# A one-core perceiver layer: steps without loops, 64-byte token list entries, a second attention by own sequence, and a new order of five steps

## What is computed

```python
def layer(x, ctx):
    # 1: cross attention with random features
    n = layernorm(x)
    K, V = ctx @ Wk + bk, ctx @ Wv + bv
    K_hat = cos(K @ Wr + br)                                   # 64 x 257 x 256
    x = x + softmax((n @ Wq + bq) @ K_hat.T) @ V
    # 2: attention inside one sequence of 32 tokens, top 8 earlier tokens by similarity
    h = layernorm(x)
    A = top8_of_strictly_earlier_tokens(h @ h.T)
    s = where(A, (h @ W_q.T) @ (h @ W_k.T).T / sqrt(32), -1e9)
    msg = softmax(s) @ h
    x = x + gelu((mix * h + (1 - mix) * msg) * gain + bias) * scale
    # 3: mixture of 8 experts, the best one for each token
    n = layernorm(x); p = softmax(n @ W_route); e = argmax(p)
    return x + max(p) * (gelu(n @ W1[e] + b1[e]) @ W2[e] + b2[e])
```

## Time and profile before

| | us |
|---|---|
| runs of before | 519.25, 520.58, 527.82 |
| median | 520.58 |
| the profiled execution's own time | 522.69 |
| its span (first to last instruction) | 520.6 |
| TensorE busy | 456.7 (88%) |
| VectorE busy | 286.1 (55%) |
| ScalarE busy | 268.8 (52%) |
| GpSimd busy | 186.8 (36%) |

### The profile page before, as it was taken

The page is one execution under the profiler, slowest core; times in us unless marked ns, Lnnn a source line. Parts: engine busy times, 40 slices in busy tenths (PEclk is TensorE's granted clock), DMA queues, the critical chain, the costliest instruction groups (busy, mean ns, idle before and its releaser), DMA issues. The chain is left out here.

```text
span 520.6 us, 10379 instructions
## 1 busy us (share of the span) xinstructions
PE 456.7 (88%) x2839; PEld 336.9 (65%) x2840; DVE 286.1 (55%) x904; ACT 268.8 (52%) x587; POOL 186.8 (36%) x326
## 2 busy tenths in 40 slices
PE   4889999999999759999999167985977999999992
PEld 3545565666666426666665055885967899999992
DVE  1556778888898548898898334763321121222220
ACT  2366768877788527788777233534213132233320
POOL 2732235334653414653545043442231332223210
PEclk9799999999999969999999768899999899999997
DMA  8612522325415305415551090353549556555300
GB/s 229 206 39 93 171 92 64 110 93 173 132 44 171 91 1 171 132 43 170 171 174 42 0 362 22 99 207 118 146 124 373 150 203 212 206 178 171 125 0 1
DMA packets 49106, 69.13 MB, mean 133 GB/s; under 512 B 8702, under 2 KB 38976, under 8 KB 48932
## 3 DMA queue, kind: packets, MB, share of 16 engines
q1 hardware_dynamic: 42820, 59.12, 34.6%
q0 software_dynamic: 3520, 8.23, 4.6%
q10 hardware_dynamic: 2720, 1.26, 0.9%
HBM read 62.20 MB, written 7.30 MB: 133 GB/s over the span
## 5 line engine op out<-in xcount | busy, mean ns | idle before, releaser
L1311 PE MATMUL pK<-stage,Wkr 128*128 128x512 f32 x256 | 126.2, 619 | 9.8 <-DVE stage L739 9.2
L1154 ACT ACTIVATE XF<-pT,b_now 128x128 f32<-128x128 f32 x184 | 52.6, 368 | 119.3 <-PE pT L1334 82.3
L1334 PE MATMUL pT<-XF,stage 128*128 128x128 f32 x736 | 92.0, 285 | 4.5 <-DMA stage<-in_L_ffn_W_dram 4.5
L1334 PEld LDWEIGHTS pT<-XF,stage 128*128 128x128 f32 x736 | 90.9, 201 | 6.9 <-issue 5.8
L1348 PE MATMUL pK<-W,XF 128*128 x368 | 87.0, 387 | 2.9 <-issue 1.3
L1348 PEld LDWEIGHTS pK<-W,XF 128*128 128x128 f32 x368 | 68.7, 193 | 12.6 <-issue 3.9
L1311 PEld LDWEIGHTS pK<-stage,Wkr 128*128 128x128 f32 x256 | 45.3, 196 | 48.7 <-issue 48.2
L356 POOL TENSOR_SCALAR ve<-mv 128x1 f32<-128x1 f32 x48 | 13.3, 276 | 157.2 <-DVE mv L662 157.1
L1135 ACT ACTIVATE stage<-pK,bkr 128x512 f32<-128x512 f32 x64 | 42.9, 689 | 34.5 <-PE pK L1311 33.0
L1142 ACT ACTIVATE stage<-stage 128x512 f32<-128x512 f32 x64 | 40.5, 633 | 20.4 <-DVE stage L734 20.2
L734 DVE TENSOR_TENSOR stage<-stage 128x512 f32<-128x512 f32 x64 | 47.7, 746 | 1.2
(11 more groups left out here) (194 smaller groups left out, 696.2 us busy)
## 6 DMA issues: line engine op xcount, KB each, us to landing
stage<-in_L_ffn_W_dram SPq DMA_DIRECT2D x23, 1024.0 KB
stage<-in_ctx_dram SPq DMA_DIRECT2D x32, 512.0 KB, 4.9
W<-in_L_ffn_W_dram SPq DMA_DIRECT2D x8, 1024.0 KB, 5.9
rows_by_token<-rows_out SPq DMA_DIRECT2D x16, 256.5 KB
ctx_last<-in_ctx_dram SPq DMA_DIRECT2D x64, 32.0 KB, 4.0
X<-in_x_dram SPq DMA_DIRECT2D x1, 1792.0 KB, 7.5
stage<-in_L_ffn_b_dram SPq DMA_DIRECT2D x1, 1024.0 KB, 9.0
token_i<-tokens_by_expert SPq DMA_DIRECT2D x23, 0.5 KB
```

Of the source, the lines that this page charges most:

```text
L1154: ins = act.activation(f_hT[b][:, n * P:(n + 1) * P], pT[i][:, (n % 4) * P:(n % 4 + 1) * P], ACT.Gelu, bias=b1_now[:, b, n:n + 1])
L1311: mm = pe.matmul(pK[r][:], Wkr[:, c, r * P:(r + 1) * P], ctx_T[:, c, half * 512:(half + 1) * 512], start=c == 0, stop=c == DC - 1)
L1334: mm = pe.matmul(pT[i][:, (n % 4) * P:(n % 4 + 1) * P], W1[q][:, c, n * P:(n + 1) * P], f_inT[:, q % 2, c * P:(c + 1) * P], start=c == 0, ...
```

## The change

1. Loops are gone: `run_steps` writes out all 21 steps, and the 16 late blocks are written out. The helpers for register values (`settle`, `in_register`, `upto`) go, and the waits on constants that `settle` made.
2. An entry of the token list is 16 int32 (64 bytes) in place of one. The start fills 1.18 MB of DRAM in place of 74 KB. `token_now`, `token_i` are 16 wide.
3. The second attention works on each sequence's own 32 columns. Similarity is 2 x 4 matmuls (128 rows, 32 x 32), scores 4 matmuls of 32 rows, `msg` 4 matmuls of 32 rows and 256 columns; queries and keys are made untransposed (64 columns), scaled in the weights, and transposed by VectorE in blocks (`qkT`); ScalarE's two copies go. All VectorE tiles there have 32 columns.
4. A new order in steps 16 to 20 on GpSimd, SyncE, VectorE and TensorE.

```diff
 def run_steps(eng, step):
-    for s in range(PEELED):
-        step(s // 2, s % 2, s // 4, s // 2 % 2)
-    with eng.Fori(0, (NG - 2 - PEELED) // 4) as i:
-        for k, half, kp in ((3 + 2 * i, 1 + i, 1), (4 + 2 * i, 2 + i, 0)):
-            step(k, 0, half, kp)
-            step(k, 1, half, kp)
-    for s in range(NG - 2, NG + STAGES):
+    for s in range(NG + STAGES):
         step(s // 2, s % 2, s // 4, s // 2 % 2)
-        by_expert = nc.dram_tensor("tokens_by_expert", [(E + 1) * TOK, 1], I32, kind="Internal").ap()
+        by_expert = nc.dram_tensor("tokens_by_expert", [(E + 1) * TOK, ENTRY], I32, kind="Internal").ap()
...
@@ gpsimd, step
                 if s in (17, 19):
-                    scatter(*routed, half - 2 + kp)
...
+                if s == 20:
+                    count_pair(routed[0])
+                    gather(5)
+                    gather(6)
...
                 if two:
                     rstd(two[0], mv2, ve2, rs2, "mv2_r", "ve2_r", "rs2_r")
                 if s == 16:
-                    gather(1)
+                    gather(0)
...
                 if s == 16:
-                    gather(2)
+                    gather(1)
+                if s in (17, 19):
+                    scatter(*routed, half - 2 + kp)
                 if four:
                     rstd(four[0], mv3, ve3, rs3, "mv3_r", "ve3_r", "rs3_r")
-                if routed and not parity:
+                if routed and not parity and s < 20:
                     count_pair(routed[0])
+                if s == 16:
+                    gather(2)
...
-                if s == 15:
-                    gather(0)
...
-                    gather(5)
-                    gather(6)
@@ sync
+                if j in FIRSTS:
+                    sp.wait_ge(S["expert_r"], FIRSTS.index(j) + 1)
-            load_tokens(0, 0, FIRSTS[1])
             sp.wait_ge(S["pv"], NG - 1)
             stream_w1(0, 0, 0)
+            load_tokens(0, 0, FIRSTS[1])
...
             keep(5, 2)
-            load_tokens(1, 3, 5)
             sp.wait_ge(S["pv"], NG)
             stream_w1(*ring(3))
+            load_tokens(1, 3, 5)
...
             keep(7, 2)
+            stream_w1(*ring(EARLY))
             load_tokens(3, EARLY, EARLY + SLOTS)
@@ vector, step
+                    v.transpose(qkT[:], p_qk).then_inc(S["qk_cp"], 1)
-                if s == 16:
-                    begin(0)
...
+                if s == 16:
+                    begin(0)
...
-                if s == 16:
-                    begin(1)
...
+                if s == 16:
+                    begin(1)
@@ tensor
-                pe.matmul(p_msg, attT[:], h[:, b, :], start=True, stop=True).then_inc(S["msg_mm"], 1)
+                for j in range(BG):
+                    own = slice(j * T, (j + 1) * T)
+                    mm = pe.matmul(p_msg[own, :], attT[own, :], h[own, b, :], start=True, stop=True,
+                                   skip_group_check=True)
...
+                    mm = pe.matmul(p_scoreB[own, :], qkT[own, 0:H], qkT[own, H:2 * H], start=True, stop=True,
+                                   skip_group_check=True)
...
                 if s == 20:
+                    up(*ring(4), 1)
                     pe.wait_ge(S["logits_r"], NG)
                     rank(routed[0])
-                    up(*ring(4), 1)
...
-                        mm = pe.matmul(p_sim, hT[:, c, :], hT[:, c, :], start=c == 0, stop=c == DC - 1)
+                        for j in range(BG):
+                            own = hT[:, c, j * T:(j + 1) * T]
+                            mm = pe.matmul(p_sim[j * T:(j + 1) * T, :], own, own, start=c == 0, stop=c == DC - 1,
+                                           skip_group_check=True)
...
-                        mm = pe.matmul(p_qk, WqkT[:, c, :], hT[:, c, :], start=c == 0, stop=c == DC - 1)
+                        mm = pe.matmul(p_qk, hT[:, c, :], WqkT[:, c, :], start=c == 0, stop=c == DC - 1)
```

More of the change, by code:

```diff
@@ L42 @@
 UNPICKED = -1.0e9
-OUTSIDE = -3.0e38
 STAGES = 5
-PEELED = 6
 def at_least(eng, sem, count):
-    if not isinstance(count, int) or count > 0:
+    if count > 0:
         eng.wait_ge(sem, count)
[L55 to L68, removed]
 def groups(k, parity, behind):
     g = 2 * k + parity - behind
-    if isinstance(g, int) and not 0 <= g < NG:
+    if not 0 <= g < NG:
         return None
@@ L82, in pair, with run_steps @@
     q = k - 3
-    if isinstance(q, int) and not 0 <= q < NG // 2:
+    if not 0 <= q < NG // 2:
         return None
     return q, 2 * ((kp + 1) % 2)
-def run_steps(eng, step):
-    for s in range(PEELED):
+def run_steps(step):
+    for s in range(NG + STAGES):
         step(s // 2, s % 2, s // 4, s // 2 % 2)
-    with eng.Fori(0, (NG - 2 - PEELED) // 4) as i:
-        for k, half, kp in ((3 + 2 * i, 1 + i, 1), (4 + 2 * i, 2 + i, 0)):
-            step(k, 0, half, kp)
-            step(k, 1, half, kp)
-    for s in range(NG - 2, NG + STAGES):
-        step(s // 2, s % 2, s // 4, s // 2 % 2)
[L100 to L112, removed]
 def perceiver_layer(nc, a, out):
@@ L587, in keep @@
                                  ).then_inc(rows_st[r0 // 2], 16)
-            for g in range(2, PEELED):
+            for g in range(2, NG):
                 next_group(g, g % 2)
@@ L939, in step @@
                     end(1)
-                if routed and not parity and (s is None or s < 18):
+                if routed and not parity and s < 18:
                     route(routed[0])
@@ L1079, in step @@
                     plan_rows(3)
-            run_steps(v, step)
+            run_steps(step)
             def late_block(j, q, turn):
-                if not isinstance(j, int) or j + 1 < NBLK:
-                    bias1(*following(j, q, turn))
-                    in_T(*following(j, q, turn))
+                if j + 1 < NBLK:
+                    bias1(*ring(j + 1))
+                    in_T(*ring(j + 1))
                 bias2(j, q, turn)
@@ L1092, in _ @@
                 end(j)
-            run_late(v, late_block)
+            for j in range(EARLY, NBLK):
+                late_block(*ring(j))
         @block.scalar
@@ L1247, in _ @@
                 late_block(*ring(j))
-            run_late(act, late_block)
+            for j in range(EARLY, NBLK):
+                late_block(*ring(j))
         @block.tensor
@@ L1528, in step @@
                     rank(routed[0])
+                if s == 16:
+                    up(*ring(0), 1)
+                    down(0, 0, (0,))
+                    in_T(*ring(1))
                 if s == 1:
```

228 lines of the change are left out of this document (107 added, 121 removed).

## The result

The changed kernel takes 481.15 us (median of 4 runs, 478.69 to 483.07) against 522.17 us beside it (519.25 to 527.82): a ratio of 0.923, 95% interval 0.915 to 0.931. The profiled execution took 483.07 us, its span 481.3 us, so the trace has 39.3 us less than the 520.6 of before.

The account below looks back on a forecast made before the run. TensorE was taken to bound full steps and late blocks, waits the stretch between; 12.3 (loops) + 0 (attention) + 22.8 (steps 16 to 20) + 8.3 (late blocks) = 43.4 us, giving 479.3 profiled, 477 at the median, range 465 to 498.

Parts of the forecast that it names:

- rival 3: Straight code stalls once where the loop's jump did, so all 12.3 us stay: 490 us; chance 0.06.
- Rival 1: Scattered 64-byte entries land no sooner, in 10 us, costing 14 us in step 16 and later blocks: 491 us; chance 0.18.
- four terms of 0.60, 0.37, 0.40 and 0.60 us: TensorE's second attention per full step: similarity, queries and keys, scores, `msg`; sum 1.97 us as before, so no gain.
- Rivals 2 and 4: Second attention: `msg` tiles run one after another, 497 us, chance 0.11; each small matmul drains the array, 540 us, chance 0.04.
- the sign of being right: Full steps of 16.2 to 16.6 us with TensorE busy throughout.
- the four named waits: TensorE idle for `h` (10.80, 3.77 us), W1 of block 0 (2.19) and `rank` (3.46) in steps 16 to 20: 20.2 us.
- The clock's 5.8 come back with the long waits: Steps 16 to 20: three half `up` slowed by low clock behind long waits recover, gaining about 5.8 us.
- the small waits: Steps 16 to 20: the rest of 16.2 us beyond the long waits, less 5.8 of clock, kept unchanged.
- three slow halves of `up`: Steps 16 to 20: halves behind waits take 3.75 and 3.65 us instead of 1.9 each, about 5.8 us of clock.
- `rank` of step 20 finds its count ready: Step 20: TensorE's 3.46 us wait ahead of `rank`, its count behind `gather(5)` and `gather(6)`, goes to 0.
- the four cases that lie over 2% below 520.6: Whole kernel faster: the forecast 0.58, rival 1 0.18, rival 2 0.11, rival 3 0.06; written as 0.95.
- the two others: Whole kernel: rival 4, slower at 540 us, chance 0.04; sums of losses that leave less than 2%, 0.03.

Follow-up runs that it names:

- no loops: The kernel before with both of its loops written out (steps 6 to 13 and the late blocks), nothing else: 509.43 us, ratio 0.976.
- the old order: The changed kernel with steps 15 to 20 in their order of before on GpSimd, SyncE, VectorE, ScalarE and TensorE: 481.82 us, ratio 0.923.
- the execution at 0.89: Profiled execution of the changed kernel with gather(5) moved ahead of the count of pair 7 in step 20: 480.88 us, ratio 0.922.
- spaced writes: The changed kernel with its 64-byte entries kept, each scatter writing only the first 4 bytes of each: 482.57 us, ratio 0.924.
- fillers: The changed kernel with 17 unread matmuls on the identity in the three gaps of step 16: 478.41 us, ratio 0.918.
- 32 bytes: The changed kernel with list entries of 32 bytes instead of 64, one run: 477.93 us.
- 16 bytes: The changed kernel with list entries of 16 bytes instead of 64, one run: 481.56 us.
- the 4-byte kernel in the old order: The changed kernel with 4-byte entries and the order of before in steps 15 to 20: 498.36 us, ratio 0.958.

## Why the prediction was right, and where not

The forecast was 477 us with 465 to 498; measured 481.15. By parts, with what the ratios give (x 521 us):

| part | predicted | measured |
|---|---|---|
| no loops | 12.3 | 12.3 |
| own sequences | 0 (-8 to +8) | 4.4 |
| landing and order together | 31.1 | 18 |
| of it landing, at the old order | not priced alone | 18 |
| of it order, with entries of 64 bytes | not priced alone | 0 |
| rest, not separated | | 5 |
| together | 43.4 | 40 |

The differences of ratios in the third column are good to some us each, so the rest of 5 is not larger than its own error.

That the sum came out within 4 us is in part luck. By place in the traces, the part up to the end of step 15 was to give 12.3 us and gave 16.9; the part behind it was to give 31.1 and gave 22.3 (17.3 to `down(4)`, 5.0 in the late blocks). Two errors of opposite sign nearly cancel.

**Part 1** held: 12.3 us by the ratio (12.4 by the length of step 10), rival 3 is dead, and the late loop shows no cost in its place. Its one run does not exclude a small one.

**Part 2** held. The landing was taken at 2.5 us. At step 15's scatter it is 2.1, at the last one, which the late blocks hang on, 4.2; the fill cost nothing at the start (first scores at 32.42 us, before 32.23). Rival 1 priced a landing of 10 us at 14 us, 491; measured it is 18 to 20, and 500.7 in the new order. The read-modify-write below 512 B of the Trainium skill (DMA: Bandwidth & Descriptors, Specifications) does not by itself give these times: 64, 32 and 16 bytes are all below 512 and their lists are there in 2.1 to 4.3 us, and 4-byte writes are fast as soon as they are spaced. If such a step exists here, its cost shows only where small writes lie close together.

**Part 3** was mis-sized, inside its bounds: four terms of 0.60, 0.37, 0.40 and 0.60 us measured 0.26, 0.50, 0.19 and 0.56. The first and the third are below their lower ends (0.43 and 0.22), so issue does not limit these small matmuls at the price that I had given it. The 0.2 us for a change of tile shape is too much too: all eight records of the scores take 0.19, and `msg` takes 0.13 beyond the 0.43 of its columns. Eight records of `msg` in 0.56 us, where one after another they would need 1.70, say that the four diagonal tiles run side by side. So the rule that different row tiles cannot access the same PSUM bank at once (the Trainium skill, TensorEngine Tiling (Array Packing), Gotcha 1: PSUM Pressure) did not serialise them here, all four writing to one bank, each to its own 32 partitions. Rivals 2 and 4 are dead by the same rows. TensorE's terms say 0.46 us a step. The step itself, from router product to router product, is 16.3 us with the full-width attention and 16.1 with the narrow one, 0.2 shorter, and that is a little below the 16.2 to 16.6 given as the sign of being right.

**Part 4** promised too much in both of its terms, waits and clock. From step 15's end to `down(4)` 57.1 us were predicted and 62.6 measured, a gain of 17.3 instead of 22.8. The windows split the missing 5.5 us. TensorE's idle time in the stretch fell from 26.1 to 11.6 us, by 14.5 where the four named waits alone were to give 17.0. Its busy time fell from 53.8 to 51.0, by 2.8 where the clock was to give 5.8.

- The step that failed is "The clock's 5.8 come back with the long waits". The long waits did go, but step 16 ran at 0.62 in the profiled execution: TensorE is busy there for 13.37 us, and for 10.04 in the execution at 0.89, whose step is 2.8 us shorter. So about 3 us of the missing 5.5 go with the clock of that execution. The four runs of the changed kernel point the same way: their mean clocks of 0.976, 0.976, 0.981 and 0.990 stand beside 483.07, 482.42, 479.89 and 478.69 us.
- The named waits came out as forecast or better: `h` 1.25 in step 16 and 1.48 in step 17, none for W1 and none for `rank`. But waits stand in four places that had none: 1.54 us for `probsT` in step 16, 0.87 and 0.51 in step 17, 0.92 ahead of `down(4)`. The forecast had carried the small waits over as they were and had added none.

The starting point of that sum was not quite right either. It takes all of the stretch but 43.5 us as waits and low clock, 36.4 us; the trace of before has TensorE idle for 26.1. The sum goes by distances from start to start; what TensorE is shown busy beyond it is the low clock and the ends of matmuls ahead of waits. The third of its three slow halves of `up` is in step 17:

```profile
324.09 3.62 PE L1334 MATMUL pT<-XF,stage 128*128 128x128 f32 x16
```

The larger error is in what the 22.8 were for. I wrote order and landing into one sum and argued most of it from the order ("`rstd` goes ahead of `gather(0)`, so `h` waits only for its own chain"). With entries of 64 bytes the old order takes 481.82 us as well: what its gather holds up is short once the list is there (2.32 us for `h` instead of 10.80). The four combinations give all of it to the landing.

For the late blocks I gained 8.3 us, and 5.0 are there, by a wait that I did not see. "`rank` of step 20 finds its count ready" is bought by putting the count, which waits for VectorE, ahead of `gather(5)`. With the one line moved the stretch is 132.33 us, where I had predicted 132.4. How much of the 3.3 us that is, the runs don't settle. With the line unmoved the stretch took 135.60 and 136.21 us in two kernels (the change, spaced writes). It took 132.22, 132.57 and 133.34 in three others (fillers, 32 bytes, 16 bytes), where the same wait was there at 0.77, 1.13 and 1.14 us and no slow half `down` followed it.

What stays open: the 4-byte kernel in the old order says that loops, attention and whatever else is left of the change make 0.042 x 521 = 22 us, of which 12.3 + 4.4 are explained. Its trace is 5.8 us shorter than that of "no loops" behind `down(4)` (134.9 against 140.7 us), and 2.1 shorter from the router product of step 15 to `down(4)`. Behind `down(4)` the traces show where: "no loops" has TensorE waiting 3.00 us for a gathered row, and both halves of the `down` behind it take 6.21 us instead of 3.62:

```profile
383.16 0.69 PE L1249 MATMUL pK<-ident,f_row 128*128 128x128 f32 x2 [3.00 <-DMA f_row<-rows_by_token,token_i]
384.01 6.21 PE L1342 MATMUL pK<-W,XF 128*128 x16 [0.16 <-issue]
```

The other has neither. Whether the narrower attention is the cause, or an interleaving of transfers that differs from execution to execution, is not shown; each was profiled once.

One slip in the chances: the four cases that lie over 2% below 520.6 sum to 0.93, where 0.95 is written, and the two others to 0.07.

## What to carry to other kernels

When a short list is scattered to DRAM and read back at once, give each entry its own 16 to 64 bytes before touching the order of anything: it was one constant and a wider buffer, worth 18 to 20 us of 521, and the reordering around it was worth nothing that the time shows. When two edits are written for each other, run all four combinations; here the one that looked like the work was worth nothing in the time. And an order that removes one wait should be read once more for what now stands behind the instruction that was moved ahead: here, in one profile of each order, 4.3 of 5.8 us were given back behind it.

## What the runs showed that I had not expected

Indirect writes of 4 bytes cost 10.2 us to land when adjacent and 3.3 us when 64 bytes apart, in the same kernel at the same place. Eight matmuls (16 records) on 128 x 32 tiles with 32 columns take 0.26 us from start to start, four (8 records) on 32 x 32 tiles 0.19. The same step 16 with the same code was granted a clock of 0.62, 0.80 or 0.89 in executions of different kernels and took 18.10, 16.95 or 15.33 us, and filling its gaps did not make it the shortest of them (17.29).
